# A macaron block on one Trainium2 core: the product of the two value weights in half-precision pairs, with both sides split in place and seven tiles of gate work ahead of it

## The reference, cut to what matters

```python
x = x + 0.5 * ffn(layernorm(x), ...)      # x: 2 x 2048 x 1024, f32
x = x + attn(layernorm(x), w_attn, w_o)   # windows of 128 tokens, squared relu, no softmax
x = x + 0.5 * ffn(layernorm(x), ...)
# attn: q, k, v = split(x @ w_attn.T); s = q k^T / 128, masked to this and the previous window
#       out = (relu(s) ** 2 @ v) @ w_o.T
# ffn:  x_norm = layernorm(x, in_gamma, in_beta)
#       thought = x_norm[last token] @ agg_w + agg_b
#       4 times: t = gelu(layernorm(thought, pn) @ d1_w + d1_b); thought += t @ d2_w + d2_b
#       out = layernorm(x + sigmoid(x @ gate_w + gate_b) * (thought @ bc_w + bc_b), out)
```

## Time and profile before

| | us |
|---|---|
| median of 3 runs | 2117.76 |
| lowest, highest | 2115.36, 2119.22 |
| profiled execution | 2117.86 |
| span of its instructions | 2116.6 |
| TensorE busy | 2037.7 |
| VectorE busy | 1173.0 |
| ScalarE busy | 664.7 |
| GpSimd busy | 159.0 |

### The profile page before, as it was taken

The page is one execution under the profiler, slowest core; times in us unless marked ns, Lnnn a source line. Parts: engine busy times, 40 slices in busy tenths (PEclk is TensorE's granted clock), DMA queues, the critical chain, the costliest instruction groups (busy, mean ns, idle before and its releaser), DMA issues.

```text
span 2116.6 us, 30247 instructions
## 1 busy us (share of the span) xinstructions
PE 2037.7 (96%) x11872; PEld 1037.0 (49%) x11872; DVE 1173.0 (55%) x2108; ACT 664.7 (31%) x931; POOL 159.0 (8%) x281
## 2 busy tenths in 40 slices
PE   8988989999999999998999999999999999999997
PEld 3333433444333446655665555665556564444443
DVE  2321323554344465567676755655555545888887
ACT  0557322433223232222333221211212113444443
POOL 0000000000000010000000000000000000111111
PEclk9999999999999999999999999999999999999999
DMA  8788897988988833348989799898987947555552
GB/s 340 237 311 341 285 353 269 379 319 320 354 338 333 332 132 118 100 140 299 323 294 327 273 320 293 297 347 283 313 290 278 357 149 221 149 151 154 154 149 80
DMA packets 275213, 555.76 MB, mean 263 GB/s; under 512 B 149040, under 2 KB 149248, under 8 KB 274688
## 3 DMA queue, kind: packets, MB, share of 16 engines
q1 hardware_dynamic: 275072, 553.83, 75.5%
HBM read 406.93 MB, written 113.26 MB: 246 GB/s over the span
## 4 chain that ended last, share of the span: by engine, by line
PE 47%; DMA 3%; DVE 2%; SPq 2%; ACT 1%; issue 1%; POOL 0%; ACTq 0%; DVEq 0%
PE product_banks L1023 41%; PE product_banks L1143 3%; PE thought_acc L1208 3%; DMA thought_units<-parts_scratch 1%; DMA gate_arena<-arena 1%; DMA arena<-in_x 0%; SPq L810 0%; DVE thought_units L1754 0%; SPq L944 0%; DMA thought_units<-in_d_w 0%; ACT arena L1315 0%; PE thought_turn L1216 0%; ACT arena L1318 0%; PE thought_acc L1198 0%; DVE arena L1566 0%
## 5 line engine op out<-in xcount | busy, mean ns | idle before, releaser
L1023 PE MATMUL product_banks<-gate_arena,arena 128*128 128x512 f16 x1536 | 354.1, 382 | 0.0
L1023 PE MATMUL product_banks<-wide_a,thought_units 128*128 128x512 f16 x1536 | 331.7, 379 | 0.0
L1023 PE MATMUL product_banks<-gate_arena,wide_a 128*128 128x256 f16 x2688 | 307.5, 274 | 2.4 <-DMA gate_arena<-arena 2.4
L1023 PE MATMUL product_banks<-wide_b,gate_arena 128*128 128x512 f16 x1344 | 301.8, 380 | 0.0
L1023 PEld LDWEIGHTS product_banks<-gate_arena,wide_a 128*128 128x128 f16 x2688 | 260.4, 98 | 59.5 <-issue 28.9
L1054 PE MATMUL product_banks<-wide_a,wide_b 128*128 128x512 f32 x512 | 240.9, 616 | 7.1 <-DMA wide_a<-in_w_attn 6.3
L1023 PEld LDWEIGHTS product_banks<-gate_arena,arena 128*128 128x128 f16 x1536 | 145.0, 98 | 203.6 <-issue 51.0
L1023 PEld LDWEIGHTS product_banks<-wide_a,thought_units 128*128 128x128 f16 x1536 | 150.3, 98 | 181.6 <-DVE arena L1606 0.5
L1023 PEld LDWEIGHTS product_banks<-wide_b,gate_arena 128*128 128x128 f16 x1344 | 127.2, 98 | 167.5 <-issue 24.9
L1423 DVE BATCH_NORM_STATS2 bn_parts<-arena 128x6 f32<-128x512 f32 x256 | 164.3, 684 | 4.4
L1054 PEld LDWEIGHTS product_banks<-wide_a,wide_b 128*128 128x128 f32 x512 | 95.1, 195 | 137.9 <-issue 137.8
(11 more groups left out here) (168 smaller groups left out, 2090.1 us busy)
## 6 DMA issues: line engine op xcount, KB each, us to landing
thought_units<-parts_scratch SPq DMA_DIRECT2D x268, 512.0 KB, 6.1
thought_units<-in_d_w SPq DMA_DIRECT2D x148, 512.0 KB, 6.7
thought_row<-in_d_w SPq DMA_DIRECT2D x76, 512.0 KB, 7.2
arena<-in_x SPq DMA_DIRECT2D x64, 512.0 KB, 8.8
parts_scratch<-thought_units SPq DMA_DIRECT2D x64, 512.0 KB, 6.2
x_scratch<-arena SPq DMA_DIRECT2D x64, 512.0 KB, 6.8
arena<-x_scratch SPq DMA_DIRECT2D x40, 512.0 KB, 6.0
gate_scratch<-arena SPq DMA_DIRECT2D x32, 512.0 KB, 8.3
```

The lines of the kernel that those rows point to most:

```text
L1023: mm = pe.matmul(bank, left(i, k), right(j, k), start=(n == 0), stop=(n == 3 * KD - 1))
```

## The change

Fold vo takes f16 pairs in place of f32. Both of its sides are split where they have landed: part e of a side is written over the f32 row e - 1, which has been used by then (part 0 goes into a spare place). The scales are found as for the other weights: a search of the largest value over eight rows of each side (`top`), then `scale_a` and `scale_b`. ScalarE's copy of a folded row applies the inverse of both scales. The early tiles are seven in place of three, and the new pieces stand beside them. The saves of gate_arena and the parameters move from fold vo into the gates behind it, where the splits of the folds now take 0.6 pieces in place of 0.3, with the saves among them. Two smaller changes of order: in fold qk the norm of tile 1 comes ahead of the turns of tile 0, at a pace of 0.9 in place of 0.8, and in the first group of the second stage the values of its first tile come ahead of the queries.

```diff
-EARLY, LATE = 3, 4
+EARLY, LATE = 7, 4
...
-        return 1.0 if piece[1:3] == ("qk", 0) else 1.83 * FOLD_SIZES[piece[2]]
+        return 1.0 if piece[1:3] == ("qk", 0) else (1.83 if piece[1] == "qk" else 1.28) * FOLD_SIZES[piece[2]]
...
+        if n == 0:
+            own = [p for p in products if p[0] == "v" and p[2] == 0]
+            products = own + [p for p in products if p not in own]
...
-    gate_rows += [("rest",), ("rest",), ("turn", 0, 0), ("turn", 0, 1), ("norm", 1)]
-    fold_qk = paced(plan_fold("qk"), gate_rows, 0.8, PE_PIECES)
+    gate_rows += [("norm", 1), ("rest",), ("turn", 0, 0), ("turn", 0, 1)]
+    fold_qk = paced(plan_fold("qk"), gate_rows, 0.9, PE_PIECES)
     fold_qk.append(("fold_store", "qk", KD - 1))
     wo = []
     for n in range(KD):
         wo += [("wv_piece", n), ("wo_turn", n, 0), ("wo_turn", n, 1)]
         if n + wo_ahead < KD:
             wo.append(("wo_rows", n + wo_ahead))
-    early = paced([p for n in range(EARLY) for p in plan_gate(n)], wo, 0.9, PE_PIECES)
-    save = [("gate_save", k) for k in range(KD)] + [("params",)] + [("rest",)] * 6 + [("half_params",)]
-    fold_vo = paced(plan_fold("vo"), save, 0.5, PE_PIECES)
-    fold_vo.append(("fold_store", "vo", KD - 1))
+        if n >= 2:
+            wo.append(("top", "wv", n - 2))
+    wo += [("top", "wv", KD - 2), ("top", "wv", KD - 1), ("scale_a", "wv"), ("rest",), ("rest",), ("scale_b", "wv")]
+    wo += [("top", "wo", e) for e in range(KD)] + [("scale_a", "wo")] + [("fold_split", "wv", e) for e in range(4)]
+    wo += [("scale_b", "wo")] + [("fold_split", "wv", e) for e in range(4, KD)]
+    wo += [("fold_split", "wo", e) for e in range(KD)]
+    early = paced([p for n in range(EARLY) for p in plan_gate(n)], wo, 1.25, PE_PIECES)
+    fold_vo = plan_fold("vo") + [("fold_store", "vo", KD - 1)]
...
+    save = [("params",)] + [("rest",)] * 5 + [("half_params",)]
+    for k in range(KD):
+        save += [("gate_save", k)] + [("rest",)] * 3
+    splits = paced(splits, save, 0.75)
     splits += [("prep_fetch", 0), ("rest",), ("rest",), ("prep_norm", 0), ("prep_beta", 0)]
-    gates = paced([p for n in range(EARLY, TILES - LATE) for p in plan_gate(n)], splits, 0.3, PE_PIECES)
+    gates = paced([p for n in range(EARLY, TILES - LATE) for p in plan_gate(n)], splits, 0.6, PE_PIECES)
...
+    fold_side = {"wv": wide_b, "wo": wide_a}
+    spare = {"wv": key_weights[:, :, :, :].rearrange("p i s t -> p (i s t)"), "wo": row_slots[0]}
+    fold_parts = lambda m, e: in_parts(fold_side[m][:, e - 1, :] if e else spare[m])
...
+                if k < ROW_RING and m == "qk":
+                    sp.wait_ge(product_full, BANK_AT[("fold", "vo", KD - 1, 1)] + 1)
...
+                    else:
+                        pe.wait_ge(side_split["wv"], e + 1)
+                        pe.wait_ge(side_split["wo"], e + 1)
...
+                    else:
+                        for n, (i, j) in enumerate(((0, 0), (0, 1), (1, 0))):
+                            mm = pe.matmul(bank_ap(key), fold_parts("wv", e)[:, i, d * P:(d + 1) * P],
+                                           fold_parts("wo", e)[:, j, h * BANK:(h + 1) * BANK], start=(e == n == 0),
+                                           stop=(e == KD - 1 and n == PARTS - 1))
...
+            elif kind == "fold_split":
+                m, e = a
+                if e == 0:
+                    act.wait_ge(scale_made, SCALE_AT[m] + 1)
+                else:
+                    act.wait_ge(side_split[m], e)
+                act.activation(fold_parts(m, e)[:, 0], fold_side[m][:, e, :], ACT.Copy,
+                               scale=scale_stat[m][:, KD + 2:KD + 3]).then_inc(side_high[m], 1)
...
+            elif kind == "fold_split":
+                m, e = a
+                dve.wait_ge(side_high[m], e + 1)
+                if e:
+                    dve.wait_ge(side_split[m], e)
+                dve.scalar_tensor_tensor(out=fold_parts(m, e)[:, 1], in0=fold_side[m][:, e, :],
+                                         scalar=scale_stat[m][:, KD + 2:KD + 3], in1=fold_parts(m, e)[:, 0],
+                                         op0=ALU.mult, op1=ALU.subtract).then_inc(side_split[m], 1)
```

More of the change, by code:

```diff
@@ L561 @@
 SPLIT_AT = {piece: n for n, piece in enumerate(p for p in PLAN if p[0] == "split")}
+SCALE_AT = {piece[1]: n for n, piece in enumerate(p for p in PLAN if p[0] == "scale_b")}
 class Tally:
@@ L1842, in gpsimd_program @@
                 m, = a
[L1843 removed]
+                pool.wait_ge(top_found, SCALE_AT[m] + 1)
                 pool.partition_all_reduce(scale_stat[m][:, KD + 1:KD + 2], scale_stat[m][:, KD:KD + 1], P,
```

51 lines of the change are left out of this document (32 added, 19 removed).

## The result

| | us |
|---|---|
| before, median of 4 runs | 2118.49 |
| after, median of 4 runs | 2146.03 |
| ratio after / before, 95% interval | 1.0133, 1.0115 to 1.0152 |
| profiled execution, its span | 2144.34, 2143.1 |

The change makes the kernel 27.5 us slower. The forecast was 2110, its range ended at 2131, and the slow rival stood at 2132: both were missed.

The account below looks back on a forecast made before the run. The prediction took TensorE, busy in 96% of the span, as the bound; fold -26.4, orders -31.0, split series +41.7 and DMA +8 sum to -7.7, giving 2110 us. Forecast range 2101 to 2119; 8 in 10, 2084 to 2131.

Parts of the forecast that it names:

- the slow rival: Tile stage: the DMA queue becomes the bound, +30 in place of +8 us, time 2132; chance 0.16.
- Fold, -26.4: Values' fold: 384 f16 matmuls at 0.2163 us take 83.0 us in place of 109.4 in f32, saving 26.4.
- The rival of a faster stream: Values' fold: matmuls stream faster than the gate's, 43.2 us in place of 83.0, time 2070; chance 0.01.
- Wait of TensorE for the series, 39: Ahead of the values' fold: splits and steps between take 65 us against TensorE's 26.5, so it stands 39 us.
- the foretold evacuation: Before the values' fold: one TensorE gap of 30 us or more, put down to VectorE's evacuation of a gate half.
- 2.7 half clock: After the wait for the split series: TensorE runs at half clock, costing 2.7 us more.
- a total of 8 us: Start of the split series: VectorE is 8 us late, from its work in the tile before and scale_b's wait.
- Changes of order, -31.0: Four reorderings: first gate 7.2, w_o transposes 8.6, saves out of the fold 8.5, values ahead of queries 6.7 us gained.
- the term for the first gate: Ahead of the first gate: the wait for tile 1's normalisation and the slow matmuls behind it go, -7.2 us.
- the one for the transposes of w_o: Tail of the w_o transposes: seven tiles place all items, so gaps and slow matmuls go, -8.6 us.
- Saves out of the fold: Values' fold: moving eight saves and two parameter loads out removes a store wait, -8.5 us, bounds 4 to 8.5.
- DMA, +8: Tile stage: denser thoughts and the saves fill the queue to 92%, lengthening waits for thought units; +8 us, bounds 0 to 18.

Follow-up runs that it names:

- order_only: Changed kernel with the values' fold left in f32 and unsplit, without its searches, scales and splits, every change of order kept: 0.9929, 2102.2 us.
- quiet_no_reduce: Changed kernel with no thought step between the first split and the values' fold, and GpSimd copying in place of reducing: 1.0107.
- before_no_reduce: Kernel before the change with GpSimd's three reductions over the partitions replaced by copies: 1.0004.
- no_reduce: Changed kernel with GpSimd's five reductions over the partitions replaced by copies: 1.0067.
- short_tops: Changed kernel with each of VectorE's 16 searches run over 64 columns in place of 1024: 1.0098.
- saves_back: Changed kernel with the eight gate saves and two parameter loads back inside the values' fold, at the pace of before: 1.0112.
- all_three: Changed kernel with 14 of 16 splits left out, GpSimd copying in place of reducing, and searches over 64 columns: 0.9920.
- spread: Changed kernel with eleven tiles of gates between the folds in place of seven and two empty places behind each split: 1.0098.

## Why the prediction was wrong, point by point

- **Fold, -26.4.** Right, mechanism and size: the work up to the second stage is 26.8 less than before and 27.4 less than in order_only. The rival of a faster stream didn't show, and so neither did the 131 ns a matmul of the Trainium skill ("TensorE: Matmul & The Clock Gate", Back-to-back issue gap), by which it would have fallen by 59, an estimate from the page's figure.
- **Wait of TensorE for the series, 39.** Right in size and in part in kind: 39.6 in three gaps, splits 2.50 us apart, and quiet_no_reduce shows that 16 splits with two normalisations fill the time alone. But the largest gap, 22.75, is for VectorE's copy of the thoughts' sums and not for the foretold evacuation, and about half of the first is GpSimd's lateness, which isn't in the sum. That the two sizes agree within 1 us is luck. The "2.7 half clock" was too small: each of three gaps has its own slow stretch, 7.7 us in this stage.
- **GpSimd.** This step failed, and with the changes of order it is the largest. The reduction of the earlier trace rows had 6.71 us of idle time ahead of it, for which the profile names no releaser. I used it as a wait of VectorE for one `scale_b`, 3 us, and never asked what is queued *behind* the reduction on GpSimd. In the changed kernel the steps behind the reductions for wo, qk and vo start 4.6, 10.4 and 7.6 us behind their data. Before, that costs nothing (before_no_reduce 1.0004), since the data of the steps behind its reductions come later than GpSimd is free. With two reductions more, and the ones for qk and vo at other places relative to the norms, it costs some 14 us (1.0133 - 1.0067 = 0.0066, and the two intervals lie apart): by stages of no_reduce, 4.7 of idle time early and 13.3 of idle time and slow clock in the gates behind the fold. Without it the time would be some 2132, still just above the range, so it isn't the only step that failed. By the Trainium skill ("GPSIMD Engine Reference", Engine selection) a reduction along the partitions belongs on GpSimd; what failed here is the order of the steps around it.
- **Searches.** I counted eight of sixteen, as lateness in one tile, within a total of 8 us. short_tops says some 7 us, at the edge of the noise. VectorE has 92.3 us of work in this stage against 48.3 in order_only, and with short searches the gap for the first normalisation falls from 8.7 to 2.8, those at 212 and 227 us for `unit_inverse` and for a copy of w_o from 1.9 and 3.4 to 0.9 and 2.5.
- **Changes of order, -31.0.** This step failed too, by 11 to 16 us. order_only measures -15 by its ratio (its interval is -21 to -9) and -20 by its span. By stages of that run against before, idle time and slow clock together: fold qk -1.9, early gates -5.5, inside the fold -11.1, the gates behind it +2.3, the rest of the kernel -4.3. The slow matmuls that follow a gap fall into the next stage's window: 2.1 us of the term for the first gate, 2.7 of the one for the transposes of w_o. Put back, the terms come out at -4.0 where I took 7.2, -6.1 where I took 8.6, -8.4 where I took 8.5, and -4.3 where I took 6.7. At the end of fold qk a gap of 2.2 for VectorE's low half took the place of the 5.0. In the early gates only the wait of 3.0 for w_o's rows is gone; the waits for its copies sum to 3.1 as before (3.0), and so do those for thought loads (5.4 and 5.2). I took each gap as gone and let nothing come next.
- **Saves out of the fold.** The size was there, the cause was wrong: with the saves back in the fold the gap stays away in both kernels, and 3 to 4 us of other waits appear. It may have belonged to how the queue met the tail of w_o's rows, or to where the sums fell; which of both wasn't tried.
- **DMA, +8.** About right in size: waits for loads of over 0.6 us sum to 11.6 us in the gates behind the fold after and 6.2 before, and to 4.1 in order_only. Since order_only has the saves in the same place, and 10.4 us remain in saves_back without them, the saves aren't what brought these waits. order_only spaces its thoughts wider, as the kernel before does; whether the spacing makes the difference wasn't tried alone. The rival, the queue as the bound of the tile stage, gave the nearest time (2132) for a cause that didn't occur: the queues moved 404 GB/s in one slice, and that stage as a whole 314 before and after. The Trainium skill's limit of about 358 ("DMA: Bandwidth & Descriptors", Where 436 GB/s comes from) is passed by that slice, as by the earlier trace rows.

The sum by spans: -20.0 for the orders (order_only), -27.4 for the fold's work, 44.4 + 7.7 in the early gates, 16.6 + 3.3 in the gates behind, and 1.8 elsewhere: +26.4, against 26.5 for the spans and 27.5 for the medians. The prediction had -31.0, -26.4, +41.7 for the early gates and +8 for the gates behind. Of the 52.1 and 19.9 us of these two stages some 14 (by the ratio) to 18 (by stages) are GpSimd's, by no_reduce; the rest of what the prediction lacked there is shown as a sum (all_three) but not traced to a step.

No run that kept the f16 fold with all of its work paid for it: the best of them, spread, stands at 1.0098. What pays is the order without it.

## What to carry to other kernels

When a change adds an operation to a rarely used engine, list what stands behind it there and who waits for that, not only who waits for its result. A series of small steps that alternates between two in-order engines can cost its length less what the bounding engine has to do meanwhile, here 39.6 us for a series of 59.7; here room between the steps only moved the wait, and two interleaved series won little. And when an edit of arithmetic comes with edits of order, measure the order alone: here it was worth 0.7% and the arithmetic cost 2%.

## What the runs showed of the hardware

GpSimd's reduction over the partitions itself takes 0.38 us (once 0.87, the first of two in a row). Between a root and a reduction the engine stood for 6.1 us or more in every kernel here, and between a reduction and the next root or thought step for 6.8 or more. Where the profile names no releaser these idle times are 6.1 to 11.3 and 6.8 to 13.2 us. They aren't the cost: part of them is time in which the data weren't there yet. Where the data came late enough, the next step followed them closely: the reduction at 244.34 in the changed kernel started 0.14 us behind its search, after 9.20 us of idle time, and the root at 409.24 in the kernel before 0.10 us behind its moments, after 8.96. So the time of the change ran while the engine waited, and only what was left of it delayed a step. Two reductions in a row followed each other at once (264.12 and 264.91). With a copy in place of the reduction it and the step behind it started within 0.1 us of their data, the copy once 0.09 us behind a root.
